# Where the loops of VectorE and ScalarE start in their instruction blocks

## Time and profile before

| | us |
|---|---|
| median of 3 runs | 2487.93 (2485.87 to 2488.28) |
| profiled execution | 2490.25 |
| its span, first to last instruction | 2488.5 |
| TensorE busy | 2227.6 (90%) |
| VectorE busy | 1749.1 (70%) |
| ScalarE busy | 1518.2 (61%) |
| GpSimd busy | 987.2 (40%) |

### The profile page before, as it was taken

One profiled execution on the slowest core, in us unless ns is written; L12 is line 12 of the kernel. 1 busy time (PEld: TensorE's weight loads), 2 busy tenths in 40 slices (PEclk: granted clock), 3 DMA queues, 4 the chain that ended last, 5 costly groups with the idle time before them and its releaser, 6 DMA issues.

```text
span 2488.5 us, 51569 instructions
## 1 busy us (share of the span) xinstructions
PE 2227.6 (90%) x14117; PEld 1847.2 (74%) x14117; DVE 1749.1 (70%) x4813; ACT 1518.2 (61%) x2926; POOL 987.2 (40%) x1301
## 2 busy tenths in 40 slices
PE   1136799999999999999999999999999999999998
PEld 1124588788887888777888878887777878788876
DVE  6936677767767777777777777777777777777664
ACT  3436567666666666666666666666666667666652
POOL 2634444334433444333444333444434444334321
PEclk7557799999999999999999999999999999999999
DMA  3211111111111121111221111111121211121211
GB/s 104 68 39 34 34 54 47 51 60 60 60 38 52 60 60 60 42 48 60 60 60 60 40 50 60 60 60 45 45 60 60 60 60 46 44 60 58 65 37 31
DMA packets 90191, 133.67 MB, mean 54 GB/s; under 512 B 20379, under 2 KB 63559, under 8 KB 90006
## 3 DMA queue, kind: packets, MB, share of 16 engines
q1 hardware_dynamic: 79176, 125.60, 17.0%
q10 hardware_dynamic: 10830, 6.35, 0.9%
HBM read 55.17 MB, written 76.74 MB: 53 GB/s over the span
## 4 chain that ended last, share of the span: by engine, by line
PE 38%; issue 33%; POOL 8%; ACT 8%; DVE 5%; POOLq 1%; DVEq 0%; ACTq 0%; DMA 0%; SPq 0%
PE bank L1449 13%; POOL CB L852 4%; PE bank L1548 3%; PE bank L1622 3%; PE bank L1538 2%; PE bank L1653 2%; POOL XD L803 2%; ACT T L879 2%; PE bank L1634 1%; PE bank L1515 1%; POOL RB L843 1%; PE bank L1504 1%; DVE VB L1144 1%; ACT CX L894 1%; PE bank L1606 1%
## 5 line engine op out<-in xcount | busy, mean ns | idle before, releaser
L1449 PE MATMUL bank<-w_hi,XHI 128*128 128x512 f32 (+1 forms) x1560 | 634.2, 407 | 1.4 <-DVE XLO L1346 1.4
L1449 PE MATMUL bank<-w_hi,XLO 128*128 128x512 f32 (+1 forms) x1560 | 558.3, 358 | 0.0
L1449 PE MATMUL bank<-w_lo,XHI 128*128 128x512 f32 (+1 forms) x1560 | 557.0, 357 | 0.0
L1097 DVE SCALAR_TENSOR_TENSOR CX<-bank,cw,CX 128x252 f32<-128x252 f32 (+5 forms) x804 | 348.4, 462 | 64.6 <-ACT CX L894 64.6
L879 ACT ACTIVATE T<-bank 64x512 f32<-64x512 f32 x256 | 151.7, 593 | 337.8 <-PE bank L1538 333.3
L1449 PEld LDWEIGHTS bank<-w_hi,XLO 128*128 128x128 f32 x1560 | 298.5, 191 | 46.8
L852 POOL TENSOR_TENSOR CB<-CB,CM 48x252 f32<-48x252 f32 (+5 forms) x402 | 265.6, 661 | 168.2 <-ACT CM L879 148.1
L1449 PEld LDWEIGHTS bank<-w_hi,XHI 128*128 128x128 f32 x1560 | 299.7, 192 | 42.8 <-DVE XLO L1346 1.6
L1449 PEld LDWEIGHTS bank<-w_lo,XHI 128*128 128x128 f32 x1560 | 299.8, 192 | 38.9
L879 ACT ACTIVATE CM<-CR,cwb 48x256 f32<-48x256 f32 x402 | 187.5, 500 | 1.6 <-POOL CB L852 1.5
L816 POOL TENSOR_TENSOR RS<-VE,half_neg 128x1 f32<-128x1 f32 x65 | 35.5, 546 | 341.8 <-DVE VE L1290 341.8
(11 more groups left out here) (294 smaller groups left out, 5405.5 us busy)
## 6 DMA issues: line engine op xcount, KB each, us to landing
carried<-T SPq DMA_DIRECT2D x65, 512.0 KB, 4.8
T<-carried SPq DMA_DIRECT2D x65, 512.0 KB, 3.9
out<-HB SPq DMA_DIRECT2D x129, 256.0 KB, 3.2
tables<-tab SPq DMA_DIRECT2D x8, 560.0 KB, 4.2
TB<-tables SPq DMA_DIRECT2D x64, 70.0 KB, 2.7
carried<-U SPq DMA_DIRECT2D x65, 64.0 KB, 3.7
XM<-carried SPq DMA_DIRECT2D x65, 64.0 KB, 4.8
XI<-in_x SPq DMA_DIRECT2D x128, 32.0 KB, 2.9
```

Of the source, the lines that this page charges most:

```text
L1097: inc(STT(CX[:, c, :, s:CS], src[:, :, 0:CS - s], cw[:, c, k:k + 1], CX[:, c, :, s:CS], ALU.mult, ALU.add), "conv")
L1449: ins = mm(bank[:, 0:c1 - c0], xs_[:, 1 - p, k, :], ws[:, k, c0:c1], start=(c0 == HID and k == 0 and n == 0), stop=(last == k and n == 2))
```

## The change

[...] The bodies, their order, and the loops of the other three engines are the same; no slot is asked for there.

```diff
             for i in range(LOOP_FROM):
                 body(i, i % 2)
-            with eng.Fori(LOOP_FROM, LOOP_TO, 2) as m:
+            slots = {eng.engine: 0} if eng in (nc.vector, nc.scalar) else None
+            with nc.Fori(LOOP_FROM, LOOP_TO, 2, engines=[eng.engine], head_slot=slots) as m:
                 for u in range(2):
                     body(m + u, u)
             for i in range(LOOP_TO, LAST):
```

## The result

| | before | after |
|---|---|---|
| median, us | 2488.11 (2485.87 to 2493.16) | 2549.12 (2522.16 to 2562.14) |
| ratio after/before | | 1.021 [1.013, 1.029] |
| profiled execution, us | 2490.25 | 2522.16 |
| its 27 loop passes, us | 1848.0 | 1881.1 |

The kernel became 2% slower, where 3.4% faster was forecast. The ratio leaves out the run of 2562.14 us, which lies over 1.5% above the fastest of the four, and the median counts it. In this version all lines behind L680 are numbered one higher, so GF's L1172 is now L1173.

The account below looks back on a forecast made before the run. TensorE bounds the kernel, kept waiting in 26 first halves by VectorE's block-load stall at the loop head. 2490.25 - 87.6 + 3.4 = 2406.1 us profiled, so 2404 forecast, own range 2398 to 2412 (2398 to 2434 with rival A).

Parts of the forecast that it names:

- Step 1: VectorE's loop head at slot 0: three blocks plus one stay, 5 loads a pass and the 2.46 us stall go.
- Step 2: The 27 loop passes: 1847.98 us become 1760.40 at 2 x 32.60 each, 87.6 less.
- rival A: TensorE in the loop: clock falls stay though the waits go; only 68.1 us gained, 2422 us; chance 0.07.
- Step 3: Entry into the loop: costs 3.4 us, added to the sum.
- Steps 4 and 5: Concern ScalarE's slot; their wording is cut. The prediction has ScalarE already looping without loads or a head gap.
- Rival B: VectorE's loop head: fewer than four blocks held after a jump, or head misplaced; nothing won, 2488 to 2491 us; chance 0.10.
- Rival C: VectorE's borders at 128th and 256th instruction: block not loaded ahead, stall costs TensorE 2.29 us a pass, 2551 us; chance 0.04.

Follow-up runs that it names:

- e8: Kernel before with VectorE's loop head at slot 100 and ScalarE's at 0, so the body touches four blocks: 2490.92 us, ratio 1.003.
- e11: Kernel before with VectorE's loop head at slot 80 and ScalarE's at 0, so the body just fits three blocks: 2417.68 us, ratio 0.967.
- e1: Kernel before with VectorE's loop head at slot 16 and ScalarE's at 0: 2411.91 us, ratio 0.968.
- e3: Kernel before with ScalarE's loop head at slot 0 and no slot asked for VectorE: 2489.09 us, ratio 1.000.
- e9: Kernel before with VectorE's loop head at slot 16 and no slot asked for ScalarE: 2412.17 us, ratio 0.965.
- e5: Kernel before with VectorE's head at slot 16, ScalarE's at 0, and two added wait calls ahead of sp_dt in first halves: 2541.10 us, ratio 1.020.
- e10: Changed kernel with GpSimd's carry of T shortened to 128 of 1024 columns, part of the computation missing: 2433.20 us, ratio 0.974 against the kernel before.
- e2: Kernel before with VectorE's loop head at slot 0 and no slot asked for ScalarE: 2548.77 us, ratio 1.022.
- e6: Kernel before, no slots set, with two added wait calls ahead of sp_dt in first halves: 2666.46 us, ratio 1.070.

## Why the prediction was wrong

- **Step 1, the stall.** Right in mechanism, size and count of blocks: q14 from 160 to 32, GF's "issue" gone but at the entry, Mt's wait gone. e8 and e11 confirm three blocks plus one. Packets are 8 KB, the steps between them 128 instructions in the mean; 383 instructions from a block's start stay (q14 at 33, e11) and 403 do not (161, e8).
- **Step 1, its last sentence: "Both waits go, and the first half becomes a second half."** This failed. Both waits went, and the first half became 36.2 us or more. I had asked what is late next only among what Mt and W depend on, within 8 us behind the head. I did not follow the shifted engine to the end of its body, where the moved border sits on an instruction that had 0.07 us of margin against GpSimd. The block borders were in the prediction's own working ("128 + 128 + 47"), and the crossing at the 128th instruction and what it sets off were priced at nothing, where the runs show 0.12 us of issue time that becomes 3.65 us of a first half. The sign was in the rows as well: the 0.63 us between the 4.52 from GF to Mt and the 3.89 of the second half come from the NF shown above, which starts inside a GpSimd instruction (1.32 us for 0.68), and I took the longer figure as a bound without asking what made it.
- **Step 2, the sum.** 87.6 us would have been nearly right: e1's 27 passes take 1767.6 us against 1763.8 in the sum with entry. The falls of the clock went with the waits, as said (1.00 in both halves of e1, against 0.95 in some of before), so rival A was wrong. In after the sum misses by 1881.1 - 1763.8 = 117.3 us: 18 first halves of some 36.25 and 7 of 37.87, one of 38.8, against 32.60 each, make 18 x 3.65 + 7 x 5.27 + 6.2 = 108.8; the entry half of 44.5 makes 44.5 - 32.6 - 3.4 = 8.5. Of a half's 3.65, 2.75 is the wait at L1505 and 0.52 that at L1480. In the longer ones the clock falls behind the wait (0.69 over the 3.2 us behind 1338.6, after 3.2 us in which TensorE was busy for 0.57), as it did in before behind another (0.55 over 3.2 us, after 3.2 us with 1.34 busy).
- **Step 3, the entry.** 3.4 predicted, 37.47 - 32.67 = 4.8 in e1, where it holds a stall of 3.8 us in place of the back edge's 2.46, and a clock of 0.95. In after it came to 11.8: GF's stall is only 2.2 us there, but the collision comes on top, and the granted clock is 0.85, so that TensorE is busy for 38.88 us with work of 32.6.
- **Steps 4 and 5.** Right: e3 and e9 put ScalarE's slot at nothing.
- **Rival B** did not occur. **Rival C**, slower, named the place, the 128th instruction, and its 2551 us lies 2 from the median, but by chance: it wanted a block that isn't loaded ahead and an "issue" wait of about 2.3 us on VectorE. Its sum also leaves the head's stall in (2487.93 + 60 + 3.4); the stall went, and with it gone the same 60 us would have given 2404 + 60 = 2464, faster than before. The runs show the block there, 0.12 us at the border, and a price made by another engine. Its chance of 0.04 was too low for another reason: an unpriced shift of one engine against another over 26 passes needs no stall to cost as much as one.

## What to carry to other kernels

Before an engine is shifted in time, look over its whole body for operations of VectorE that miss one of GpSimd by a tenth of a microsecond and are of the kind that was held here (sp_aa, NM and NF: two inputs in SBUF, 0.68, 3.12 and 1.32 us in place of 0.16, 0.15 and 0.68), and take a duration that is 20 times its usual (NM, 3.12 for 0.15) as the sign that they met. A VectorE loop whose body touched three blocks of 128 instructions loaded nothing in its passes, and one that touched four loaded five in each (the difference is worth 3.2% of the time here, e1), but the borders have to be put where 0.12 us does not change the order of two engines: try two or three slots that hold the body in as many blocks, as 0, 16 and 80 here (2549, 2412, 2418 us).

## What the runs showed of the hardware

- VectorE looped without loading when its body touched three blocks of 128 instructions (8 KB each; q14 at 32 in after, 33 in e11), and loaded five a pass when it touched four (160 before, 161 in e8); in these two kernels a jump back cost 2.5 us in the mean (2.8 at most) before, and 2.1 (2.2 at most) in e8.
- Crossing a border into a block that is there cost VectorE 0.12 us of issue time at the 128th instruction (after) and at the 48th (e11), 0.06 us just ahead of the 256th (after), and nothing that shows at the 112th and 240th (e1).
- sp_aa, 128 x 16 elements with two SBUF inputs, takes 0.16 us, or 0.68 when it starts 0.05 us behind the start of a GpSimd addition (after), and 0.58 when it starts 0.15 behind (e5). NM, 128 x 1 with two SBUF inputs too, takes 0.15 us (up to 0.26 before); held, it took 0.32 (e10), 3.1 or 4.1 (after, e2, e5, e6), and what decides between these was not shown. HWS, with one input in PSUM, takes 0.27 or 0.28 us inside an addition and is not held; sp_dt, with two in SBUF, takes 0.17 or 0.18 inside GpSimd's RS.
- 0.22 us on one engine cost 6.8 us a pass in the mean, the low clock of TensorE included (e6).
